# Context term as one fp32r matmul, W2 prepared bank by bank, fewer lookups ahead, seven unread matmuls: a DLRM tower kernel on one core

## The reference

```python
e = jnp.stack([tbl_0[ids[:, 0]], ..., tbl_38[ids[:, 38]]], axis=1)     # (1024, 39, 16)
def _cin_layer(x0, xk, W, b):
    out = jnp.einsum('bhd,bmd,shm->bsd', xk, x0, W) + b[None, :, None]
    return jax.nn.relu(out)
x1 = _cin_layer(e, e, W1, b1)          # W1 (128, 39, 39)
x2 = _cin_layer(e, x1, W2, b2)         # W2 (128, 128, 39)
z = jnp.concatenate([x1.sum(axis=-1), x2.sum(axis=-1)], axis=-1)
h = jnp.concatenate([z, dense_ctx], axis=1)          # 256 + 16 columns
h = jnp.maximum(h @ W_top1 + b_top1, 0.0)            # 512
h = jnp.maximum(h @ W_top2 + b_top2, 0.0)            # 256
y = h @ W_top3
```

## Time and profile before

| | |
|---|---|
| median of 3 runs | 1210.94 us (1210.28 to 1210.98) |
| the profiled execution | 1209.32 us; its span 1207.3 us |
| TensorE (PE) busy | 96% |
| VectorE (DVE) busy | 89% |
| GpSimd (POOL) busy | 75% |
| ScalarE (ACT) busy | 57% |
| mean granted TensorE clock | 0.991 |

### The profile page before, as it was taken

One profiled execution on the slowest core, in us unless ns is written; L12 is line 12 of the kernel. 1 busy time (PEld: TensorE's weight loads), 2 busy tenths in 40 slices (PEclk: granted clock), 3 DMA queues, 4 the chain that ended last, 5 costly groups with the idle time before them and its releaser, 6 DMA issues.

```text
span 1207.3 us, 18938 instructions
## 1 busy us (share of the span) xinstructions
PE 1162.2 (96%) x4952; PEld 898.9 (74%) x4952; DVE 1075.3 (89%) x3811; ACT 692.3 (57%) x2177; POOL 900.6 (75%) x930
## 2 busy tenths in 40 slices
PE   3897999999999999999999999999999999999998
PEld 2575777777777777777777677777778777777766
DVE  4476899999999999999999779999999999999966
ACT  3554565656666556666565555566666566656432
POOL 7898998888888888888887676888876454645432
PEclk9998999999999999999999999999999999999998
DMA  5111111111111111111111100111110000000000
GB/s 180 8 7 7 7 8 6 7 6 7 6 7 8 7 6 7 6 6 7 7 7 6 6 5 5 7 7 7 7 6 2 1 1 1 1 1 1 1 1 1
DMA packets 170249, 11.58 MB, mean 10 GB/s; under 512 B 163630, under 2 KB 169262, under 8 KB 170013
## 3 DMA queue, kind: packets, MB, share of 16 engines
q1 hardware_dynamic: 159901, 7.73, 7.5%
q0 software_dynamic: 10240, 2.64, 2.8%
HBM read 7.92 MB, written 0.00 MB: 7 GB/s over the span
## 4 chain that ended last, share of the span: by engine, by line
PE 59%; DVE 16%; ACT 12%; issue 6%; POOL 6%; DMA 0%; POOLq 0%; DVEq 0%; ACTq 0%; SPq 0%
PE ps L881 16%; PE ps L882 15%; DVE acc L769 15%; PE ps L885 14%; ACT fy L552 9%; POOL looked L422 4%; PE ps L914 3%; PE ps L837 2%; ACT ps L585 2%; ACT zh L584 1%; PE ps L850 1%; PE ps L851 1%; PE ps L853 1%; PE ps L825 1%; POOL fsum L431 1%
## 5 line engine op out<-in xcount | busy, mean ns | idle before, releaser
L769 DVE SCALAR_TENSOR_TENSOR acc<-ps,e,acc 128x128 f32<-128x128 f32 x3186 | 846.9, 342 | 76.6 <-PE ps L885 70.6
L431 POOL TENSOR_TENSOR fy<-fy 128x512 f32<-128x512 f32 (+1 forms) x256 | 403.0, 1574 | 204.7 <-ACT fy L552 196.3
L881 PE MATMUL ps<-w2h,x1h 128*128 128x512 f32 (+1 forms) x1280 | 523.3, 409 | 21.2 <-ACT fy L552 9.9
L882 PE MATMUL ps<-w2l,x1h 128*128 128x512 f32 (+1 forms) x1280 | 496.3, 388 | 0.0
L885 PE MATMUL ps<-w2h,x1l 128*128 128x512 f32 (+1 forms) x1280 | 495.5, 387 | 0.4 <-DVE x1l L721 0.4
L552 ACT ACTIVATE fy<-ps,e 128x128 f32<-128x128 f32 x1536 | 415.8, 387 | 83.0 <-PE ps L885 82.9
L422 POOL DMA_INDIRECT looked<-in_table,rows x320 | 311.6, 974 | 58.3 <-POOL fy L431 23.4
L881 PEld LDWEIGHTS ps<-w2h,x1h 128*128 128x128 f32 x1280 | 241.5, 189 | 125.9 <-DVE acc L769 33.9
L885 PEld LDWEIGHTS ps<-w2h,x1l 128*128 128x128 f32 x1280 | 241.1, 188 | 49.6 <-DVE x1l L721 0.9
L882 PEld LDWEIGHTS ps<-w2l,x1h 128*128 128x128 f32 x1280 | 241.7, 189 | 43.7 <-issue 4.7
L584 ACT ACTIVATE zh<-ps 128x512 fp32r<-128x512 f32 x168 | 103.7, 617 | 247.2 <-PE ps L837 243.2
(11 more groups left out here) (87 smaller groups left out, 624.4 us busy)
## 6 DMA issues: line engine op xcount, KB each, us to landing
e<-looked SPq DMA_DIRECT2D x360, 5.0 KB, 1.9
looked<-in_table,rows POOLq DMA_INDIRECT x320, 2.4
e<-looked SPq DMA_DIRECT2D x120, 4.5 KB, 1.9
w_st<-in_w SPq DMA_DIRECT2D x1, 1728.0 KB, 10.1
wt_sb<-in_wt SPq DMA_DIRECT2D x2, 512.0 KB, 4.1
w_st<-in_w SPq DMA_DIRECT2D x1, 768.0 KB, 5.9
w_sb<-in_w1a SPq DMA_DIRECT2D x1, 448.0 KB, 3.2
w1b_sb<-in_w1b SPq DMA_DIRECT2D x1, 448.0 KB, 3.9
```

The costliest lines, as they stand in the source:

```text
L431: nc.gpsimd.tensor_tensor(out, a, b, ALU.add).then_inc(s_fsum, 1)
L769: nc.vector.scalar_tensor_tensor(acc[:, sub, :] if m < fields("D", last)[-1] else y, y, emb(p, sub, m), acc[:, sub, :] if m else fsum[:, p ...
L881: nc.tensor.matmul(y, x1h[:, t % 2, at], w2h[:, cols], start=True, stop=False)
L882: nc.tensor.matmul(y, x1h[:, t % 2, at], w2l[:, cols], start=False, stop=False)
```

## The change

1. `SOON` goes from 4 to 6: tiles 4 and 5 also have the unsplit first layer, with steps every 2 slots. `LATE` goes from 4 to 7: pairs 4 to 6 also add `fsum` at their end.
2. `lookups(p)`: 6 in pair 0, 5 in pairs 1 to 3, 6 from pair 4 on (before 7 in pairs 0 to 5, then 6).
3. `high_slots`: ScalarE's two staging steps move from slots 0 and 1 to slots 1 and 4 for tiles under `SOON`, and to 4 and 5 for tile 3 (pair 2). In pair 2 POOL does the low parts ahead of the first addition.
4. `e_hl` has 4 buffers for 8; its memset is half as long.
5. VectorE's W2 work is cut into pieces of one bank, and TensorE waits for the pieces of its bank alone.
6. The context's rows and weights are laid out three times in the rows 0, 32 and 64 of an 80-row tile (DMAs of 320 KB and 160 KB for 64 and 32 KB); ScalarE rounds both (in pair 14), VectorE makes the low part in one copy each (ends of pairs 16 and 18), and the three products become one fp32r matmul of 80 rows for two fp32 instructions.
7. Behind the fold of W1 TensorE does seven fp32 matmuls of 512 columns into a PSUM bank that nobody reads.

```diff
-SOON = 4
+HELD = 4
+SOON = 6
-LATE = 4
+LATE = 7
+WARM = 7
 def lookups(p):
-    return 7 if p < 6 else 6
+    return 6 if p == 0 or p >= 4 else 5
 def high_slots(p):
-    return (6, 7) if p == 0 else (0, 1) if SPLIT_IN[p] < SOON else (3, 6)
+    return (6, 7) if p == 0 else (4, 5) if p == 2 else (1, 4) if SPLIT_IN[p] < SOON else (3, 6)
+CONTEXT_AT, CONTEXT_LOW = (14, 9), (16, 18)
...
-        e_hl = sb("e_hl", [P, LOOKED, P, DT])
+        e_hl = sb("e_hl", [P, HELD, P, DT])
...
+                    if p == 2:
+                        low_parts(nc.gpsimd, mine)
                     if then < PAIRS:
                         middle_fields(then)
                     look_ahead(1)
-                    if mine_soon:
+                    if mine_soon and p != 2:
                         low_parts(nc.gpsimd, mine)
...
+                def context_high():
+                    act.wait_ge(s_mlpw, 16 * len(mlp_weights))
+                    nc.scalar.activation(ctx_r[:], ctx_sb[:], ACT.Copy).then_inc(s_ctxh, 1)
+                    nc.scalar.activation(wt1c_r[:], wt1c_sb[:], ACT.Copy).then_inc(s_ctxh, 1)
...
+                def context_low():
+                    rows = slice(CTX_ROWS[1], CTX_ROWS[1] + CTX)
+                    dve.wait_ge(s_ctxh, 1)
+                    nc.vector.tensor_tensor(ctx_r[rows, :], ctx_sb[rows, :], ctx_r[rows, :], ALU.subtract).then_inc(s_ctxl, 1)
...
                 dve.wait_ge(s_w2h, 1)
-                w2_low(slice(MD * S, M * S))
+                for j in range(A_BANKS):
+                    w2_low(columns("A", j))
                 dve.wait_ge(s_w2d, 16)
-                nc.vector.tensor_scalar(w2h[:, 0:MD * S], w2_st[:, 0:MD * S], 0.5, None, ALU.mult).then_inc(s_w2h, 1)
-                dve.wait_ge(s_w2h, 2)
-                w2_low(slice(0, MD * S))
+                for j in range(D_BANKS + 1):
+                    if j < D_BANKS:
+                        cols = columns("D", j)
+                        nc.vector.tensor_scalar(w2h[:, cols], w2_st[:, cols], 0.5, None, ALU.mult).then_inc(s_w2h, 1)
+                    if j:
+                        dve.wait_ge(s_w2h, 1 + j)
+                        w2_low(columns("D", j - 1))
...
+                    if p == 0:
+                        pe.wait_ge(s_w2l, A_BANKS if kind == "A" else A_BANKS + j + 1)
...
                         terms = [(wt1_sb[:, 0, f], p1[:, lo:hi]), (wt1_sb[:, 1, f], p2t[:, lo:hi]),
-                                 (wt1c_sb[:, f], ctx_sb[:, lo:hi])]
+                                 (wt1c_r[:, f], ctx_r[:, lo:hi])]
...
                 mm.then_inc(s_fold, 1)
+                for _ in range(WARM):
+                    nc.tensor.matmul(ps[:, 0, :], ident_sb[:], w1_sb[:, 1:5, :].rearrange("p c s -> p (c s)"), start=True, stop=True)
```

More of the change, by code:

```diff
@@ L18 @@
 CTX = 16
+CTX_ROWS = (0, 32, 64)
+CTX_K = CTX_ROWS[-1] + CTX
 F1, F2 = 512, 256
@@ L87, in fields, with columns @@
     return range(MD + MB * j, min(MD + MB * j + MB, M))
+def columns(kind, j):
+    return slice(fields(kind, j).start * S, fields(kind, j).stop * S)
 def d_banks(p):
@@ L296, in cin_tower @@
         s_mlpw = sem("s_mlpw")
+        s_ctxh = sem("s_ctxh")
+        s_ctxl = sem("s_ctxl")
         s_rows = sem("s_rows")
@@ L369, in low_parts @@
         def low_parts(engine, t):
-            done, hl = s_el_first if t < FIRST_TILES else s_el, e_hl[:, t % LOOKED, :, :].rearrange("p m d -> p (m d)")
+            done, hl = s_el_first if t < FIRST_TILES else s_el, e_hl[:, t % HELD, :, :].rearrange("p m d -> p (m d)")
             engine.wait_ge(s_eh, 3 * t + 1)
@@ L605, in high_part @@
                     wait_put(act, t)
-                    if t >= LOOKED:
-                        act.wait_ge(s_full, STAGED["turn", t - LOOKED] + 1)
-                    nc.scalar.activation(e_hl[:, t % LOOKED, 0:M, :].bitcast(F32R), e[:, t, :, :], ACT.Copy).then_inc(s_eh, 1)
+                    if t >= HELD:
+                        act.wait_ge(s_full, STAGED["turn", t - HELD] + 1)
+                    nc.scalar.activation(e_hl[:, t % HELD, 0:M, :].bitcast(F32R), e[:, t, :, :], ACT.Copy).then_inc(s_eh, 1)
                 def products_high(t):
@@ L618, in products_high @@
                     for row in (ZH, ZW):
-                        nc.scalar.activation(e_hl[:, t % LOOKED, row:row + ZP, :].bitcast(F32R), src, ACT.Copy).then_inc(s_eh, 1)
+                        nc.scalar.activation(e_hl[:, t % HELD, row:row + ZP, :].bitcast(F32R), src, ACT.Copy).then_inc(s_eh, 1)
+                def context_high():
+                    act.wait_ge(s_mlpw, 16 * len(mlp_weights))
+                    nc.scalar.activation(ctx_r[:], ctx_sb[:], ACT.Copy).then_inc(s_ctxh, 1)
+                    nc.scalar.activation(wt1c_r[:], wt1c_sb[:], ACT.Copy).then_inc(s_ctxh, 1)
                 def sums_turned(t):
@@ L717, in square_low, with context_weights_low @@
                     nc.vector.tensor_tensor(zl[:, k % 2, :], ps[:, BK_T, :], zh[:, k % 2, :], ALU.subtract).then_inc(s_zl, 1)
+                def context_low():
+                    rows = slice(CTX_ROWS[1], CTX_ROWS[1] + CTX)
+                    dve.wait_ge(s_ctxh, 1)
+                    nc.vector.tensor_tensor(ctx_r[rows, :], ctx_sb[rows, :], ctx_r[rows, :], ALU.subtract).then_inc(s_ctxl, 1)
+                def context_weights_low():
+                    rows = slice(CTX_ROWS[2], CTX_ROWS[2] + CTX)
+                    dve.wait_ge(s_ctxh, 2)
+                    nc.vector.tensor_tensor(wt1c_r[rows, :], wt1c_sb[rows, :], wt1c_r[rows, :], ALU.subtract).then_inc(s_ctxl, 1)
                 def first_layer_low(t):
@@ L776, in _ @@
                             square_low(*at)
+                    if p == CONTEXT_LOW[0]:
+                        context_low()
+                    elif p == CONTEXT_LOW[1]:
+                        context_weights_low()
                     for sub in range(2):
@@ L825, in turn @@
                         mm = nc.tensor.transpose(ps[:, BK_T, d * P:(d + 1) * P],
-                                                 e_hl[:, t % LOOKED, :, d], ident_sb[:])
+                                                 e_hl[:, t % HELD, :, d], ident_sb[:])
                     mm.then_inc(s_full, 1)
@@ L957, in _ @@
                     nc.tensor.matmul(ps[:, TAIL_1[c], 0:n], wt1_sb[:, 0, f], p1[:, lo:hi], start=True, stop=False)
-                    nc.tensor.matmul(ps[:, TAIL_1[c], 0:n], wt1c_sb[:, f], ctx_sb[:, lo:hi], start=False, stop=False)
+                    nc.tensor.matmul(ps[:, TAIL_1[c], 0:n], wt1c_r[:, f], ctx_r[:, lo:hi], start=False, stop=False)
                 sums(TILES - 1)
@@ L1025 @@
     first_row = np.repeat(first_row.reshape(LOOKUPS, Q).T, BT, axis=0)
+    wt1c, ctx_t = np.zeros((CTX_K, F1), np.float32), np.zeros((CTX_K, B), np.float32)
+    for row in CTX_ROWS:
+        wt1c[row:row + CTX], ctx_t[row:row + CTX] = x["W_top1"][2 * S:], x["dense_ctx"].T
     arrays = {
```

15 lines of the change are left out of this document (10 added, 5 removed).

## The result

The changed kernel takes 1192.31 us (median of four runs, 1191.50 to 1196.69) against 1210.96 of the kernel before (four runs, 1210.28 to 1211.69). The ratio is 0.9853, 95% interval 0.9828 to 0.9878, so 18.6 us less; the forecast was 1194.4. The profiled execution took 1191.93, 17.4 less than that of the kernel before, which was 1.6 under its median.

A forecast was written before the change was run, and what follows sets the result against it. TensorE and VectorE, nearly equally loaded, were taken to bound the steady part, with time lost in stops elsewhere. Terms -3.0 - 9.1 - 0.7 - 5.0 + 1.2 + 0.1 = -16.5 took 1210.9 to 1194.4 us; range 1190.5 to 1201.

The forecast's parts named there:

- The opening: Start of the kernel: shorter W2 pieces release tile 1's lookups earlier, and seven matmuls raise TensorE's clock; -3.0 us.
- the one that I left to the range: Opening: TensorE's remaining stop lasts 1.3 us; if that leaves the clock up, 1.6 us more are gained.
- The hole: TensorE's stop near 93 us, at tile 3's staging: earlier products and banks drained before waits remove it; -9.1 us.
- Rival B: Part of the hole returns at tile 3, 4 or 6 because POOL waits for ScalarE; 1199 us, chance 0.10.
- Tiles 4 and 5 and the late sums: Unsplit first layers and field sums at pair ends: less VectorE work, slightly more TensorE work, TensorE-bound; -0.7 us.
- The context: MLP blocks: one fp32r matmul replaces the fp32 context term, 1.05 us becoming 0.23 plus perhaps 0.1, eight blocks; -5.0 us.
- The low parts: VectorE's two context subtractions in the nearly full steady part cost between nothing and 1.9 us; taken as +1.2.
- One pair more with lookups: Later in the kernel, lookups extend over one more pair; costs 0.1 us.
- A: Rival: the opening gives nothing, as lookups delay VectorE's pieces or the seven matmuls run late; 1197.4 us, chance 0.17.
- D: Rival: slower; with fewer lookups ahead, ScalarE waits for copies in each tile from 6 on; 1228 us, chance 0.03.
- E: Rival: hole and opening gain nothing, context gain paid for by VectorE work and tiles 4 and 5; within 0.2%, chance 0.02.
- C: Rival: more is gained, as no lookup stands and the clock stays up, 2.0 + 1.6 more; 1190.8 us, chance 0.06.

The follow-up runs named there:

- w2_low_whole: Changed kernel with VectorE's W2 low parts in two long instructions, the high part still in pieces; 1203.15 us, ratio 0.9902 to the kernel before.
- no_warm_again: Changed kernel without the seven unread matmuls, run again on another chip; 1193.91 us, ratio 0.9866 to the kernel before.
- after_again: The changed kernel itself, unedited, run once more on another chip; 1192.89 us, ratio 0.9857 to the kernel before.
- lookups_old: Changed kernel with the old number of lookups, 7 in pairs 0 to 5, then 6; 1197.56 us, ratio 0.9899 to the kernel before.
- ctx_early_late9: Changed kernel with the context's rounding in pair 0, its low parts in pairs 0 and 1, and LATE 9 for 7; 1212.98 us, ratio 0.9982 to before.
- soon4: Changed kernel with SOON back at 4, so tiles 4 and 5 are split again; 1221.34 us, ratio 1.0052 to the kernel before.
- ctx_fp32: Changed kernel with the context term back to two fp32 instructions, without rounding copies and low parts; 1216.97 us, ratio 1.0012 to the kernel before.

## Why the prediction was right, step by step

**The opening, forecast -3.0, measured -4.74.** The mechanism held for the lookups. The last lookup of tile 1 started at 28.44 (forecast 29.3), the seven matmuls ended at 20.09 (about 20), `x1h` came at 29.41 (29.3) and `put(1)` at 31.05 (near 31.8). `w2_low_whole` shows that each long instruction holds one lookup, and the pieces do not. The six lookups took 1.1 us more than six of 0.95, where I had counted some 0.35 each for five. The mis-sized step is the one that I left to the range: the stop was 0.39 and not 1.3, so the clock stayed up, and the 1.6 us for that came in full: 3.0 + 1.6 = 4.6. I had split the gain wrongly in one point. I gave the seven matmuls 0.6 us because a stop for `put(1)` followed. That stop is nearly gone, so what they save at the transposes and behind them counts in full: 1.0 to 1.7 us (`no_warm_again`). That all of tile 0 ran at the upper level, which the forecast took for granted, was in part luck: in `after_again` TensorE idled for 2.23 us behind the seven matmuls and worked at the lower level again, and tile 1 comes at 55.42 for 53.39. About 2 us of the opening's gain are not there in each execution.

**The hole, forecast -9.1, measured -9.12** between tiles 1 and 3. Products at 90.46 (forecast 91.3), no wait left at either `e_hl` row. VectorE's 9.04 us of waiting and TensorE's 9.3 both fit: it was time lost by two engines that never catch up. Rival B did not occur in the changed kernel, but `lookups_old` is just B: POOL's debt moved from tile 3 to tile 5, as a wait of 5.25 us for field sums.

**Tiles 4 and 5 and the late sums, forecast -0.7, measured +1.09.** This is the step that failed, in sign. I reckoned a tile "TensorE-bound, 0.6 less than 34.88 at best", from busy times. The four windows of the changed kernel against those of before, with `ctx_early_late9`, take it apart. An unsplit tile takes 35.11 or 35.10 us where a split one takes 34.88, although VectorE has 2.4 us less to do (31.1 for 33.5): +0.23 for each, +0.46 together. The turn back from late sums, in the first pair past `LATE`, costs 1.02 in tile 5's stretch (36.12 for 35.10): VectorE waits 1.29 us there, at 170.16, for POOL's field sums. As I read it they are late because POOL is staging a tile in the pair ahead; the run shows only that the wait is gone with `LATE` = 9. I had priced the late sums as work and not as a wait. The stretch with 159 matmuls takes 0.39 less (36.14 for 36.53). That is +1.09. The unsplit tile is bound by TensorE, as I had it (34.6 of its 35.1 us busy), but at 35.1 and not at my count of 34.3; where the 0.8 goes stays open. What I missed altogether is what the unsplit tiles are good for. They are a date for the copies, worth 13 us by `soon4` with this kernel's lookups.

**The context, forecast -5.0, measured -7.3.** The new term is what the forecast said: 0.23 for 1.05, by the chain, so 0.82 a block. I had called this the upper end. The lower end of 0.63 does not follow from my own terms (1.05 less 0.23 less the 0.1 of a switch is 0.72), so the -5.0 was taken out of a range that was too low: 0.72 to 0.82, for eight blocks, four of them at 7/8, is -5.4 to -6.2. What I left out stood ahead of and behind the old term. From the start of the block's first matmul to the next product it is 0.91 less in a block of 512 columns and 0.83 less in one of 448, 7.0 for the eight, and the product behind a context term then took 0.34 to its successor where it now takes 0.24 (656.40 to 656.74, 645.37 to 645.61), up to 0.8 more. Nothing was gained at the `p2t` matmuls. `ctx_fp32` gives 7.2 from the other side.

**The low parts, forecast +1.2, measured +2.54** between tiles 6 and 12, 2.28 by `ctx_fp32`. In a part where VectorE is nearly full the upper end of the row's price (1.9) was the one to take: TensorE's stops of 1.21 and 0.68 are just as long. What the other 0.4 to 0.6 us is stays open.

**One pair more with lookups, forecast +0.1, measured +0.55** over tiles 19 to 31, 0.38 of it in the one tile that now has them. The rest is within what traces of one program differ by: over the same tiles `after_again` takes 422.06 us, the changed kernel 422.59 and the kernel before 422.04. Forecast sum -16.5, measured -17.2: +1.8, +1.3 and +0.45 lost against the forecast, -1.7 and -2.3 won, and -0.2 over the steady tiles. The single errors are larger than their sum. Rivals A, D and E did not occur. Of C, the clock came and the full release of the lookups did not.

## What to carry to other kernels

Where two engines are nearly full, price a long idle gap, and new work given to one of them, at its whole length: the hole's 9.04 us came back as 9.1, and 1.9 us of low parts cost 2.3 to 2.5. A low-part subtraction with both inputs in SBUF has no fixed length; look at what GpSimd runs beside it before moving it, and cut such instructions up where GpSimd's list is the clock. Before costing an edit by its work, look for the dates that it sets: `SOON` looked like a trade of some tenths and held 13 us. And a start recorded behind an fp32 matmul can lie inside it, so price a term there from the whole block.
